# GpSimd's addition of x and bias put behind the wait for the slots, in front of the four sends, with three buffers of rows

## The reference

```
x = layernorm(x + attention(x))          # 16 heads of 16, rope, causal softmax, projection W_proj, b_proj
logits = tokens @ gate_w.T               # 8 experts
probs  = softmax(logits); e = argmax(probs)
rank   = place of the token among those of its expert, in order; kept if rank < 640
ans    = probs[e] * (relu(token @ w1[e] + b1[e]) @ w2[e] + b2[e])   # as reference: the sum over tec, ecd
x = layernorm(x + ans)                   # ans is 0 for a token that is not kept
```

## Time and profile before

| | us |
|---|---|
| median of 3 runs | 1352.88 |
| lowest, highest | 1350.56, 1355.76 |
| profiled execution | 1350.51 |
| its span | 1348.6 |
| gating stage | about 955 to 1084 |

### The profile page before, as it was taken

The page is one execution under the profiler, slowest core; times in us unless marked ns, Lnnn a source line. Parts: engine busy times, 40 slices in busy tenths (PEclk is TensorE's granted clock), DMA queues, the critical chain, the costliest instruction groups (busy, mean ns, idle before and its releaser), DMA issues. The chain is left out here.

```text
span 1348.6 us, 22141 instructions
## 1 busy us (share of the span) xinstructions
PE 1239.5 (92%) x7669; PEld 618.8 (46%) x7669; DVE 1130.6 (84%) x2612; ACT 772.6 (57%) x1082; POOL 278.6 (21%) x382
## 2 busy tenths in 40 slices
PE   7997999999999999999999999999677469999996
PEld 4552233333333333333333333332366369999996
DVE  7989999999999999999999999992488548888886
ACT  3541267667667667667667667668344444454452
POOL 3344011111111111111111111111444501111221
PEclk9996699999999999999999999999877679999998
DMA  5694342302302202302302300121356223333330
GB/s 181 180 210 118 49 47 53 85 12 53 85 11 53 87 9 53 91 5 53 91 5 53 89 7 30 45 68 56 102 149 212 106 85 120 116 108 106 101 111 18
DMA packets 99471, 108.34 MB, mean 80 GB/s; under 512 B 18588, under 2 KB 88095, under 8 KB 99360
## 3 DMA queue, kind: packets, MB, share of 16 engines
q1 hardware_dynamic: 95776, 98.46, 27.4%
q0 software_dynamic: 3584, 8.47, 1.8%
HBM read 72.60 MB, written 40.26 MB: 84 GB/s over the span
## 5 line engine op out<-in xcount | busy, mean ns | idle before, releaser
L612 ACT ACTIVATE probs<-scores 128x1024 f32<-128x1024 f32 (+3 forms) x640 | 539.0, 895 | 290.7 <-PE scores L453 290.2
L715 DVE TENSOR_REDUCE part_max<-ring 128x1 f32<-128x512 f32 x768 | 477.9, 683 | 23.5 <-PE ring L493 23.1
L493 PE MATMUL ring<-k_stack,q_stack 96*128 96x512 bf16 (+3 forms) x1280 | 400.6, 362 | 10.6 <-ACT v_s L582 4.9
L453 PE MATMUL scores<-q_stack,k_stack 99*128 99x512 bf16 (+3 forms) x1280 | 338.6, 349 | 8.3 <-DMA q_stack<-max_rows 5.7
L473 PE MATMUL out_p<-probs,v_s 128*17 128x512 f32 (+3 forms) x2560 | 295.7, 534 | 0.5 <-POOL probs L782 0.3
L493 PEld LDWEIGHTS ring<-k_stack,q_stack 96*128 96x128 bf16 x1280 | 114.0, 97 | 308.4 <-DVE part_max L715 146.1
L709 DVE CUSTOM_DVE_ANT_0 scratch<-ring,mask_s 128x384 f32<-128x384 f32 (+2 forms) x384 | 196.5, 554 | 32.1 <-PE ring L493 29.0
L453 PEld LDWEIGHTS scores<-q_stack,k_stack 99*128 99x128 bf16 x1280 | 112.6, 98 | 182.6 <-issue 57.0
L782 POOL TENSOR_SCALAR_AFFINE_SELECT probs<-probs 128x512 f32<-128x512 f32 x128 | 81.2, 635 | 396.5 <-ACT probs L612 380.5
L1383 PE MATMUL psY<-w_hi,h_hi 128*128 128x256 f32 x320 | 90.9, 284 | 0.0
L1417 ACT ACTIVATE h_whole<-psH,b_s 128x384 f32<-128x384 f32 (+1 forms) x128 | 66.9, 528 | 41.5 <-PE psH L1364 33.7
(11 more groups left out here) (116 smaller groups left out, 1378.0 us busy)
## 6 DMA issues: line engine op xcount, KB each, us to landing
w_whole<-w SPq DMA_DIRECT2D x16, 1024.0 KB, 6.3
q_stack<-pieces_d SPq DMA_DIRECT2D x192, 64.0 KB, 2.9
k_stack<-pieces_d SPq DMA_DIRECT2D x168, 64.0 KB, 3.1
o_d<-o_s SPq DMA_DIRECT2D x32, 256.0 KB, 2.3
slots_d<-no_row SPq DMA_DIRECT2D x8, 650.0 KB, 6.1
xe<-slots_d SPq DMA_DIRECT2D x8, 650.0 KB
xin<-x SPq DMA_DIRECT2D x8, 512.0 KB, 5.0
pieces_d<-hi SPq DMA_DIRECT2D x32, 128.0 KB, 3.4
```

Of the source, the lines that this page charges most:

```text
L453: last = nc.tensor.matmul(scores[p][:, hh, off:CHUNK], k_stack[i][0:KROWS, kb // TPC, j, kb % TPC * P:(kb % TPC + 1) * P], q_stack[i][0:KR ...
L493: last = nc.tensor.matmul(slot[:, h * w:(h + 1) * w], q_stack[i][0:SROWS, qt // TPC, j + h, qt % TPC * P:(qt % TPC + 1) * P], k_stack[i][0 ...
L612: nc.scalar.activation(probs[n % NPROB][:, 2 * p:2 * p + 2, off:CHUNK], scores[p][:, :, off:CHUNK], ACT.Exp, scale=SCALE).then_inc(exp_don ...
L715: nc.vector.tensor_reduce(part_max[:, qt, j, t:t + 1], ring[m % 3][:, 0:w], axis=AX.X, op=ALU.max).then_inc(ring_read, 1)
```

## The change

Three edits, all in project_and_gate.

1. POOL's order. The wait for the slots is taken out of send and put in front of the addition: for each n slots_known(n), then add_bias(n+2), then send(n). The additions of chunks 0 and 1 still stand ahead of all.
2. rows and slot_index have three buffers (NROWS = 3) in place of two, used by n % 3; so have the semaphores rows_sent, with one primer DMA each. rows(n) now waits for send(n-3), and for the plain rows of chunk n-3.
3. What goes with that: three memsets of the rows' last columns, and counts adapted.

```diff
-            def send(n, i):
+            def slots_known(n):
                 done = in_register(pool, 1 + (n + 1))
                 pool.wait_ge(w_loaded, 16 * (n_w - 1))
                 pool.wait_ge(slots_ready, done)
+
+            def send(n):
                 for t in range(TPC):
                     nc.gpsimd.indirect_dma_start(
...
             add_bias(0, 0, 0)
             add_bias(1, 1, 0)
-            for k in range(0, NC3 // 2 - 1):
-                add_bias(2 * k + 2, 0, k + 1)
-                send(2 * k, 0)
-                add_bias(2 * k + 3, 1, k + 1)
-                send(2 * k + 1, 1)
-            for n in (NC3 - 2, NC3 - 1):
-                send(n, n % 2)
+            for n in range(NC3):
+                slots_known(n)
+                if n + 2 < NC3:
+                    add_bias(n + 2, n % 2, n // 2 + 1)
+                send(n)
...
-                dve.wait_ge(rows_sent[i], 16 + 16 * TPC * h)
-                if not (isinstance(n, int) and n == 0):
-                    dve.wait_ge(plain_ready, 1 + TPC * (n - 1))
+                dve.wait_ge(rows_sent[n % NROWS], 16 + 16 * TPC * (n // NROWS))
+                if n >= NROWS:
+                    dve.wait_ge(plain_ready, 1 + TPC * (n - NROWS + 1))
...
-        rows = [sb(f"rows{i}", [P, TPC, RW]) for i in range(2)]
+        rows = [sb(f"rows{i}", [P, TPC, RW]) for i in range(NROWS)]
...
-        slot = [sb(f"slot_index{i}", [P, TPC], U32) for i in range(2)]
+        slot = [sb(f"slot_index{i}", [P, TPC], U32) for i in range(NROWS)]
```

More of the change, by code:

```diff
@@ L802 @@
 NOWHERE = 1.0e6
+NROWS = 3
 TILES = B * T // P
@@ L828, in project_and_gate @@
         eps_s = sb("eps_s", [P, 1])
-        primer = sb("p3_primer", [2, P])
+        primer = sb("p3_primer", [NROWS, P])
         count_s = sb("count_s", [P, E])
@@ L894, in project_and_gate @@
         slots_ready = sem("slots_ready")
-        rows_sent = [sem(f"rows_sent{i}") for i in range(2)]
+        rows_sent = [sem(f"rows_sent{i}") for i in range(NROWS)]
         NC3 = B * NCH
@@ L965, in project, with turn_x1 @@
                     last.then_inc(projected, 1)
-            def turn_x1(n, i):
+            def turn_x1(n):
                 pe.wait_ge(rows_ready, TPC * (n + 1))
@@ L973, in turn_x1 @@
                         last = nc.tensor.transpose(psD[:, kt, t * P:(t + 1) * P],
-                                                   rows[i][:, t, kt * P:(kt + 1) * P], id_s[:])
+                                                   rows[n % NROWS][:, t, kt * P:(kt + 1) * P], id_s[:])
                 last.then_inc(x1_turned, 1)
@@ L1003, in _ @@
             for n in range(NC3):
-                turn_x1(n, n % 2)
+                turn_x1(n)
                 gate_logits(n)
@@ L1038, in plain_rows @@
                 for t in tiles:
-                    nc.scalar.activation(plain[i][:, t, :], rows[i][:, t, 0:C], ACT.Copy,
+                    nc.scalar.activation(plain[i][:, t, :], rows[n % NROWS][:, t, 0:C], ACT.Copy,
                                          scale=rstd2[i][:, t:t + 1]).then_inc(plain_ready, 1)
@@ L1055, in _ @@
             nc.vector.memset(count_s[:], 0.0).then_inc(set_up, 1)
-            for i in range(2):
+            for i in range(NROWS):
                 nc.vector.memset(rows[i][:, :, C:RW], 0.0).then_inc(set_up, 1)
-            dve.wait_ge(set_up, 4)
+            dve.wait_ge(set_up, 2 + NROWS)
             dve.wait_ge(w_loaded, 16 * (n_w - 1))
@@ L1084, in residual, with norm_chunk @@
                 done = in_register(dve, m + 1)
-                dve.wait_ge(set_up, 4)
+                dve.wait_ge(set_up, 2 + NROWS)
                 dve.wait_ge(stat_ready, done)
                 nc.vector.bn_aggr(mv[i][:, t, :], stats[t % 2][:]).then_inc(mv_ready, 1)
-            def norm_chunk(n, i, h):
+            def norm_chunk(n, i):
                 dve.wait_ge(std_ready, n + 1)
@@ L1097, in norm_chunk @@
                 nc.vector.tensor_tensor(var2[i][:], var1[i][:], rstd[i][:], ALU.mult).then_inc(var_step, 1)
-                dve.wait_ge(rows_sent[i], 16 + 16 * TPC * h)
-                if not (isinstance(n, int) and n == 0):
-                    dve.wait_ge(plain_ready, 1 + TPC * (n - 1))
+                dve.wait_ge(rows_sent[n % NROWS], 16 + 16 * TPC * (n // NROWS))
+                if n >= NROWS:
+                    dve.wait_ge(plain_ready, 1 + TPC * (n - NROWS + 1))
                 for t in range(TPC):
-                    nc.vector.tensor_scalar(rows[i][:, t, 0:C], res[i][:, t, :], mv[i][:, t, 0:1],
+                    nc.vector.tensor_scalar(rows[n % NROWS][:, t, 0:C], res[i][:, t, :], mv[i][:, t, 0:1],
                                             rstd[i][:, t:t + 1], ALU.subtract, ALU.mult).then_inc(rows_ready, 1)
@@ L1132, in choose, with place @@
                 nc.vector.tensor_tensor(onehot[:], wanted[:], per_tile(best[:]), ALU.is_equal).then_inc(onehot_ready, 1)
-            def place(n, i):
+            def place(n):
                 dve.wait_ge(onehot_ready, n + 1)
@@ L1142, in place @@
                 wait_step(n, 5)
-                step(n, 7, nc.vector.reciprocal(rows[i][:, :, PROB], total[:]))
+                step(n, 7, nc.vector.reciprocal(rows[n % NROWS][:, :, PROB], total[:]))
                 dve.wait_ge(ranks_ready, n + 1)
@@ L1146, in place @@
                                                    ALU.add))
-                step(n, 9, nc.vector.tensor_copy(rows[i][:, :, TOKEN], token_s[:]))
+                step(n, 9, nc.vector.tensor_copy(rows[n % NROWS][:, :, TOKEN], token_s[:]))
                 wait_step(n, 8)
@@ L1158, in place @@
                 wait_step(n, 15)
-                nc.vector.tensor_tensor(slot[i][:], slot1[:], dropped[:], ALU.add).then_inc(slots_ready, 1)
+                nc.vector.tensor_tensor(slot[n % NROWS][:], slot1[:], dropped[:], ALU.add).then_inc(slots_ready, 1)
             normalise(0)
@@ L1165, in _ @@
                 residual(0, 0, t)
-            norm_chunk(0, 0, 0)
+            norm_chunk(0, 0)
             for n in range(1, NC3):
@@ L1174, in _ @@
                 choose(n - 1)
-                norm_chunk(n, i, n // 2)
-                place(n - 1, 1 - i)
+                norm_chunk(n, i)
+                place(n - 1)
             norm_plain(NC3 - 1, 1)
             choose(NC3 - 1)
-            place(NC3 - 1, 1)
+            place(NC3 - 1)
         @block.gpsimd
         def _(pool):
-            for i in range(2):
+            for i in range(NROWS):
                 nc.gpsimd.dma_start(primer[i:i + 1, :], ident[i:i + 1, :]).then_inc(rows_sent[i], 16)
@@ L1201, in send @@
                 pool.wait_ge(slots_ready, done)
+            def send(n):
                 for t in range(TPC):
                     nc.gpsimd.indirect_dma_start(
-                        slots_d, bass.IndirectOffsetOnAxis(ap=slot[i][:, t:t + 1], axis=0),
-                        rows[i][:, t, :], None, bounds_check=E * CAP - 1, oob_is_err=False,
-                    ).then_inc(rows_sent[i], 16)
+                        slots_d, bass.IndirectOffsetOnAxis(ap=slot[n % NROWS][:, t:t + 1], axis=0),
+                        rows[n % NROWS][:, t, :], None, bounds_check=E * CAP - 1, oob_is_err=False,
+                    ).then_inc(rows_sent[n % NROWS], 16)
             add_bias(0, 0, 0)
             add_bias(1, 1, 0)
-            for k in range(0, NC3 // 2 - 1):
-                add_bias(2 * k + 2, 0, k + 1)
-                send(2 * k, 0)
-                add_bias(2 * k + 3, 1, k + 1)
-                send(2 * k + 1, 1)
-            for n in (NC3 - 2, NC3 - 1):
-                send(n, n % 2)
-            for i in range(2):
-                pool.wait_ge(rows_sent[i], 16 + 16 * TPC * NC3 // 2)
+            for n in range(NC3):
[3 more added lines that the diff above has]
+                send(n)
+            for i in range(NROWS):
+                pool.wait_ge(rows_sent[i], 16 + 16 * TPC * len(range(i, NC3, NROWS)))
 def experts(nc, slots_d, w_whole, w1, b1, w2, b2, ident, out_d):
```

## The result

| | before | changed |
|---|---|---|
| median, us | 1353.54 | 1365.21 |
| lowest to highest | 1350.56 to 1357.36 | 1363.52 to 1367.05 |
| runs | 5 | 5 |
| profiled execution | 1350.51 | 1364.85 |

The changed kernel takes 1.0083 times as long, with a 95% interval of 1.0065 to 1.0101: it is 11 us slower by this ratio and 11.7 us by the medians, where 11.5 were forecast (1364.4 us).

The account below looks back on a forecast made before the run. A loop of dependences (residual, yT, project, ranks, place) was taken to set the gating stage's turn. -0.5 + 15.9 - 1.5 - 2.4 = +11.5 us, forecasting 1364.4 us against the median; range 1357 to 1370 us.

Parts of the forecast that it names:

- The loop: Gating stage's chunk turn: residual start to PE start 5.54, project 6.69, project's end to next residual 1.31, together 13.54 us.
- Part 1: VectorE's stall in wanted beside GpSimd's addition goes, but lay on the loop only in iteration 6: -0.5 us.
- Part 2: VectorE's residual for chunks 2 to 7 waits for the addition, now behind the slots: 6 x 2.65 = +15.9 us.
- Rival C: The wait for the addition is dearer, 3.4 us each, with PE's clock at its worst: +20.4, 1373.3 us; 11%.
- Part 3: Third buffer of rows removes VectorE's wait for send(5) before writing rows(7) in iteration 7: -1.5 us.
- Part 4: PE's clock: the five projects of iterations 2 to 6 take 5.9 us each, 29.5 against 31.9: -2.4 us.
- Rival B: New wait exists, but PE regains full clock, five projects at 3.4 us each: -1.0, 1351.9 us; 6% for within noise.

Follow-up runs that it names:

- Run 3: Changed kernel with three xb buffers and GpSimd's addition made one chunk further ahead (n+3 in place of n+2); ratio to before 0.9991.
- run 4: Project halved (one of two products per tile left out) with GpSimd's old order, addition ahead, and new order: 1344.5, 1334.8 and 1350.9 us.
- run 1: Changed kernel with GpSimd's order as before, leaving only the third buffer of rows; ratio to before 0.9986, -1.9 us.
- run 5: Kernel with the addition one chunk ahead, plus five or three idle PE matmuls in front of project; ratios to before 0.9909 and 0.9927.
- run 2: Changed kernel with two buffers of rows in place of three, new order kept; ratio to before 1.0085.
- run 6: Ranks put behind project's first tile, with GpSimd's addition ahead, old order and new order: 1334.4, 1344.5 and 1348.6 us.

## Why the prediction was right

- **The loop** (5.54 + project + 1.31): right. After, turn less project is 9.51 to 9.53 us in iterations 2 to 6 (14.92 - 5.39 is the first); before it was 6.85 (13.54 - 6.69). The difference, 2.67, is the wait alone. The prediction didn't name the second loop, over GpSimd, of 12.38 us; it counted only in iteration 6.
- **Part 1, -0.5**: right. Iteration 6 lost the 0.5 us that its stall had cost; elsewhere the 2.68 us went into rank_all's wait. Run 3 shows it, run 4 shows why. The 0.5 us hung on a project of 5.10 us in that one execution: with the same order in run 1 project took 6.78 there, and the stall cost nothing.
- **Part 2, +15.9**: right, 6 x 2.67 = 16.0. The start of the addition took 0.14 us, as in the earlier trace rows, and not the 0.85 us of a send. The sends do start 0.16 us after the addition. Rival C is out.
- **Part 3, -1.5**: the wait is gone, and iteration 7 grew by 2.67 - 1.57 = 1.10 us. That nothing else of the third buffer counts held for this kernel. With two buffers a wait of 2.92 us in iteration 5 appears that I had not worked out, and it cost 0.5 us.
- **Part 4, -2.4**: the five projects took 5.39, 6.46, 5.31, 6.41 and 5.29 us, 28.9 against 31.9: -3.0. That the middle of slow and fast came near was luck: it had no reason in the prediction, and nothing in it said that long and short would alternate. With the same order and two buffers they were 6.68, 5.42, 6.47, 5.32 and 6.15 us, 30.0 together, so this term is good to a us or so. Rival B is out: PE's gap before project is 5.28 us and no project ran at 2.4 GHz throughout. Rival B's 3.4 us for such a project was too low as well: run 5 measured 3.72 to 3.74, since the 6.8 us that were halved had already run partly at the higher level.
- **What I left out**: iteration 1 grew by 1.1 us. turn_x1 took 1.97 us for 1.18 (granted clock 0.50 for 0.87), so its logits and its project started 0.8 us later within it, and project took 6.61 for 6.33. It is hardly the change: run 2 has the same order there, and its iteration 1 took 13.57 us, as before (13.56). The sum over iterations 2 to 7 was +11.0 for +11.5 forecast; with iteration 1 and the ends it is 12.4 in the stage, and 11.7 in the medians.

## What to carry to other kernels

Before moving work out of an engine's stall, ask who that engine waits for next: if a wait stands behind the stall, the stall is already paid for there. And put a prefetching instruction behind a semaphore only after finding in the other engine's order what stands right behind the instruction that raises it; here it was the very consumer. One more buffer of xb with the addition a chunk further ahead has neither the stall nor the wait, but by itself it gained nothing that the runs can tell from zero (0.9991). The gain lay in the order of PE's instructions: project was half of the turn (6.69 of 13.54 us), and the ranks that VectorE waited for stood behind it. Only then was the stall worth removing, and its price was not its length but the loop that it closed over GpSimd.

## What the runs showed of the hardware that I had not expected

- A VectorE instruction with two inputs in SBUF that met GpSimd's addition ended 0.06 us after it, wherever it had begun (run 6, old order: rows of 1.14 to 2.72 us for the same work). The stall is better read as a wait for the addition's end than as a fixed cost.
- The same 16 matmul rows of project take 3.7 to 6.8 us by where in them the granted clock steps up. Four of the five projects before took 6.57 to 6.77 us; with the new order 5.3 and 6.4 alternated, and with three filler matmuls 6.1 to 6.4 and 3.72. The turn's length follows from it (turn less project is constant for one order), and what decides where the step falls is not shown here; a sum that takes one length for all turns can be off by 1.5 us a turn.
- With two buffers and the new order, the sends issued from 1037.68 to 1042.51 us in iteration 5 held VectorE until 1047.57. SP had issued the 2 MB of weights at 1037.97, beside them; before, the last send of iteration 7, issued by 1060.79, had let go by 1062.38. That the weights were the cause was not tried by itself.
